# Four slot lanes by groups, rows of the second expert stage stored straight into the output, and places read when a block's rows arrive, in a conditioned transformer with two expert stages

## The chip, the cores and the metric

One Trainium2 chip, one of its cores. The metric is the device time of one execution in microseconds (us); lower is better. A core has TensorE (PE; PEld are its weight loads), VectorE (DVE), ScalarE (ACT), GpSimd (POOL) and SyncE (SP), which here only issues DMAs. Every engine works through its own instructions in order and waits on semaphores. Matrix products land in PSUM (the eight tensors `bank[0..7]`), everything else on chip is in SBUF (`sb_...`). All data is float32.

## The reference

Sixteen batch entries of 128 tokens with 128 features (2048 tokens, 16 tiles of 128x128).

```python
# layer 0: conditioned block, then experts
x = attention(adaln1(x)) + x ; x = cross_attention(adaln2(x), ctx) + x ; x = geglu(adaln3(x)) + x
z = layernorm(x); x = x + shared_ffn(z) + sum over the top 2 of 7 experts: w_k * ffn_k(z)
# layer 1: slot attention over the 77 context rows, 3 rounds, then experts
S = start from layernorm(x)                          # 128 slots per batch entry
for _ in range(3):
    q = layernorm(S); att = softmax over the slots; att = att / its row sums
    mid = S + update(att, values)                    # wu, bu
    S = layernorm(mid + w2 . gelu(w1 . layernorm(mid)) + ...)   # lnp_g, lnp_b
x3 = x + S ; z = layernorm(x3)
out = x3 + w * ffn_e(z), e the best of 8 experts, w its softmax share
```

## The kernel before

**Phase 1** (to about 550 us) runs layer 0's attention blocks as a software pipeline over the 16 tiles, iterations -1 to 17, stage B of tile b in iteration b + 1. The values of the cross attention go through DRAM: ACT fills `v2_rows`, SP stores them to `v2_all` (`store_values`) and loads tile b's part into `v2` (`load_values`), where PE waits for them in `pv_pair` by the semaphore `v2_in`. SP issues in program order, in the function `_(sp)`: the loads of inputs, `values(0)`, then two copies from DRAM to DRAM, `rows_a<-pad_a` and `rows_b<-pad_b`, that fill the tables of expert rows with padding, then `values(1)` to `values(15)`. In `load_values(b)` SP waits first until the stores it needs have landed. All these transfers are on SP's one queue.

**Stage a** (to 673 us): the first experts. Tokens are scattered to `rows_a` by expert; 38 blocks of 128 rows are loaded, multiplied, and sent back by `send_back("a", back_a)` on POOL. **Slots** (680 to 877 us): `back_a` is added to x, and the sixteen tiles go in two lanes of eight tiles (`LANES = ((0, 1), (2, 3))`, groups of four tiles), three rounds of `slot_round`. In a round DVE takes per lane statistics (`measured`: bn_stats, bn_aggr), POOL the power -1/2 (`root`), DVE the shift (`nbias`), ACT normalises (`normed`), PE turns the tiles (L893), ACT scales them (L1162), PE makes the logits (L903), DVE the maxima, ACT the exponentials (L1183), DVE the shares (L1748), PE the update (L911), DVE adds it (L1763), the same statistics and turn again, PE layer 1 (L923), ACT gelu (L1194), PE layer 2 (L929), DVE adds the rest (`mlp_sums`, L1783), measures and scales (`scaled`, L1713 and L1720). The order on each engine is that in which the calls stand in `slot_round`; PE, ACT, DVE and POOL run it in a hardware loop. POOL also keeps `s_rest` (L2057, L2063) and adds half of `back_a`.

**Routing b** (877 to 886 us): `routing("b", 0)` on DVE for all 16 tiles. POOL then scatters 16 tiles to `rows_b`, SP loads blocks. **Stage b** (910 to 963 us): 23 blocks: `turn_rows`, 4 products, ACT relu, 4 products, DVE bias (`leave`), and POOL in `send_back("b", back_b)`: `meta<-blk_x` (L2004), `dest<-meta` (L2011), an indirect DMA (L2016). **Tail**: SP loads `back_b` into `picked`, DVE multiplies by `wgt1` and adds x, SP stores `out`.

Of the kernel before, what the change touches and what calls it, by code (L numbers as in the profile page):

```python
# [32 lines left out]
NREG = EA * REGION + NR - 2 * TOK // P  # L33

PARTS = {"a": ((0, 12), (12, B)), "b": ((0, B),)}
SLOT_ITERS = 3
ROW = D + 2
NSLOT = 4
# [44 lines left out]

RANK_AT = [last + 2 for _, last in PARTS["a"][:-1]]

# [90 lines left out]
def program(nc, A, row_names, out):  # L176
    PLAN = proj_plan()
    with ExitStack() as ctx:
# [35 lines left out]
        start_a = sb("start_a", 1, NR, dt=I32)  # L214
# [63 lines left out]
        picked = sb("picked", P, B, 2, D)  # L278
# [6 lines left out]
        blk_x = sb("blk_x", P, NSLOT, ROW)  # L285
        meta = sb("meta", P, NR, 2)
        dest = sb("dest", P, NSLOT, dt=I32)
# [7 lines left out]

        rows_a = nc.dram_tensor("rows_a", (NREG * P, ROW), F32, kind="Internal").ap()
        rows_b = nc.dram_tensor("rows_b", (NB * P, ROW), F32, kind="Internal").ap()

        back_a = nc.dram_tensor("back_a", (2 * TOK + NREG * P, D), F32, kind="Internal").ap()
        v2_all = nc.dram_tensor("v2_all", (B * C, INNER), F32, kind="Internal").ap()  # L300
        back_b = nc.dram_tensor("back_b", (TOK + NB * P, D), F32, kind="Internal").ap()
# [19 lines left out]
        def quads(t):  # L321
# [25 lines left out]
        out_sem = sem("out_sem")  # L347
# [14 lines left out]
        meta_kept, dest_ready = ({x: sem(n + x) for x in "ab"} for n in ("meta_kept_", "dest_ready_"))  # L362
        sent_ready = sem("sent_ready")
# [9 lines left out]
        x2_step = sem("x2_step")  # L373
        sl_step, sl_var, sl_root = sem("sl_step"), sem("sl_var"), sem("sl_root")
        statq_ready, statm_ready, stat3_ready = (
            sem("sl_" + n) for n in ("statq_ready", "statm_ready", "stat3_ready"))
        zqT_done, zqT_ready, lg_done, nmax_ready, att_exp, att_ready, upd_done, mid_ready, mid_rest = (
            sem("sl_" + n) for n in ("zqT_done", "zqT_ready", "lg_done", "nmax_ready", "att_exp",
                                     "att_ready", "upd_done", "mid_ready", "mid_rest"))
        zmT_done, zmT_ready, hid_done, hid_ready, mlp_done, sum_ready, S_ready, S_rest = (  # L380
            sem("sl_" + n) for n in ("zmT_done", "zmT_ready", "hid_done", "hid_ready", "mlp_done",
# [12 lines left out]
        def tiles(lane):  # L394
            return range(4 * LANES[lane][0], 4 * LANES[lane][-1] + 4)
# [140 lines left out]
        def _(pe):  # L536
# [359 lines left out]
            def slot_logits(it, lane):  # L896
                for g in LANES[lane]:
                    turn_group(g, zq_ready, it * G + g + 1, zqT_done)
# [1259 lines left out]
```

## Time and profile before

| | us |
|---|---|
| median of 3 runs | 981.83 (980.21 to 982.06) |
| profiled execution: its time | 977.38 |
| its span, first to last instruction | 975.6 |
| busy: PE / DVE / ACT / POOL | 770.0 / 584.4 / 509.1 / 388.4 |
| chain that ended last, by engine | PE 46%, DVE 21%, issue 14%, POOL 9%, ACT 5% |

The span is the time from the first to the last instruction of the one profiled execution; 1.8 us of that execution lie around it. The chain that ended last is followed back from the last instruction, at each step to what released it.

### The profile page before, as it was taken

The page shows a single profiled execution, that of the slowest core. Times are in us where ns is not written, and L with a number is a line of the kernel's source. Part 1 is how long each engine was busy: PE and PEld are TensorE (multiplying, and loading weights), DVE is VectorE, ACT ScalarE, POOL GpSimd, SP SyncE. Part 2 cuts the span into 40 slices and gives each one's busy share as a digit, 9 for nine tenths or more (in the row PEclk, how much of TensorE's full clock was granted, in tenths as well). Part 3 has the DMA queues.
Part 4 walks back from the last instruction along what each step waited for, and adds up shares of the span by engine and source line. Part 5 has one row for each costly group of instructions (what it writes and reads, how often), then busy time and mean ns, then how long its engine had stood idle before and what let it go on. Part 6 is the DMA issues. An engine that isn't in the chain of part 4 may idle for free.

```text
span 975.6 us, 18523 instructions
## 1 busy us (share of the span) xinstructions
PE 770.0 (79%) x5945; PEld 650.1 (67%) x5945; DVE 584.4 (60%) x1939; ACT 509.1 (52%) x1078; POOL 388.4 (40%) x563
## 2 busy tenths in 40 slices
PE   5898899999999999999777699999363645550692
PEld 5677778788888788887665459998242534340692
DVE  2477778777767666568754443333869687763012
ACT  2566677666677666676444223335364545530461
POOL 1234354333333333332337333656624344225453
PEclk9799999999999999999897799999677677765796
DMA  9592011000011001010001136885300000002463
GB/s 264 182 352 94 1 36 36 14 23 28 2 35 36 15 16 34 2 35 28 14 6 37 68 99 174 253 244 167 106 1 1 0 0 0 0 1 76 127 198 106
DMA packets 43155, 70.95 MB, mean 73 GB/s; under 512 B 5339, under 2 KB 28587, under 8 KB 42651
## 3 DMA queue, kind: packets, MB, share of 16 engines
q1 hardware_dynamic: 39579, 62.64, 21.1%
q0 software_dynamic: 3488, 7.20, 2.1%
q8 instruction: 48, 0.79, 0.3%
q14 instruction: 40, 0.33, 0.1%
HBM read 56.53 MB, written 22.67 MB: 81 GB/s over the span
## 4 chain that ended last, share of the span: by engine, by line
PE 46%; DVE 21%; issue 14%; POOL 9%; ACT 5%; DMA 2%; SPq 2%; DVEq 0%; POOLq 0%; ACTq 0%
PE bank L568 5%; PE bank L839 5%; PE bank L630 5%; PE bank L593 3%; DVE sb_smax L1376 3%; PE bank L583 3%; DVE sb_row_sum L1386 3%; PE bank L618 3%; PE bank L574 2%; PE bank L602 2%; PE bank L847 2%; PE bank L659 2%; PE bank L970 2%; DVE sb_st_all L1680 2%; POOL sb_rstd_all L2052 2%
## 5 line engine op out<-in xcount | busy, mean ns | idle before, releaser
L1954 POOL TENSOR_TENSOR sb_expd<-sb_expd,sb_rden 128x512 f32<-128x512 f32 (+1 forms) x128 | 112.6, 880 | 270.3 <-DVE sb_rden L1390 270.1
L1376 DVE TENSOR_REDUCE sb_smax<-bank 128x4 f32<-128x512 f32 (+1 forms) x128 | 74.1, 579 | 63.6 <-PE bank L593 38.8
L618 PE MATMUL bank<-sb_eye,sb_expd 128*128 128x128 f32 (+1 forms) x512 | 78.2, 280 | 6.9 <-POOL sb_expd L1954 6.2
L1080 ACT ACTIVATE sb_expd<-sb_shifted 128x512 f32<-128x512 f32 (+1 forms) x128 | 69.8, 545 | 21.0 <-DVE sb_shifted L1379 19.6
L1386 DVE TENSOR_REDUCE sb_row_sum<-sb_expd 128x4 f32<-128x512 f32 (+1 forms) x128 | 72.9, 570 | 10.9 <-ACT sb_expd L1080 10.9
L1074 ACT ACTIVATE sb_probT<-bank 128x512 f32<-128x512 f32 (+1 forms) x128 | 74.3, 590 | 9.1 <-PE bank L618 8.8
L618 PEld LDWEIGHTS bank<-sb_eye,sb_expd 128*128 128x128 f32 (+1 forms) x512 | 59.9, 146 | 28.3 <-POOL sb_expd L1954 13.9
L1379 DVE TENSOR_TENSOR sb_shifted<-bank,sb_smax 128x512 f32<-128x512 f32 (+1 forms) x128 | 74.9, 585 | 4.4
L893 PE MATMUL bank<-sb_eye,sb_z_all 128*128 128x128 f32 x96 | 24.3, 420 | 66.9 <-ACT sb_z_all L1168 66.9
L568 PE MATMUL bank<-sb_h1T,sb_watt 128*128 128x128 f32 x512 | 72.6, 289 | 4.5 <-DMA sb_watt<-att_w 2.3
L630 PE MATMUL bank<-sb_probT,sb_v 128*64 128x128 f32 (+1 forms) x1024 | 71.2, 282 | 5.5 <-issue 4.0
L568 PEld LDWEIGHTS bank<-sb_h1T,sb_watt 128*128 128x128 f32 x512 | 64.6, 199 | 9.1 <-DVE sb_xb L1365 3.6
L1168 ACT ACTIVATE sb_z_all<-sb_S,sb_nbias,sb_rstd_all 128x128 f32<-128x128 f32 x84 | 33.6, 481 | 62.0 <-DVE sb_nbias L1707 62.0
L630 PEld LDWEIGHTS bank<-sb_probT,sb_v 128*64 128x64 f32 (+1 forms) x1024 | 55.6, 138 | 14.6 <-issue 5.4
L893 PEld LDWEIGHTS bank<-sb_eye,sb_z_all 128*128 128x128 f32 x96 | 17.5, 214 | 71.5 <-ACT sb_z_all L1168 71.2
L2052 POOL TENSOR_TENSOR sb_rstd_all<-sb_rsq_all,sb_halves 128x8 f32<-128x8 f32 x22 | 36.7, 1669 | 59.2 <-DVE sb_rsq_all L1695 59.1
L839 PE MATMUL bank<-sb_blk_xT,sb_up_w 128*128 128x128 f32 x456 | 57.1, 275 | 0.0
L839 PEld LDWEIGHTS bank<-sb_blk_xT,sb_up_w 128*128 128x128 f32 x456 | 54.0, 192 | 0.0
L2016 POOL DMA_INDIRECT back_a<-sb_blk_y,sb_dest x38 | 37.1, 976 | 40.0 <-DVE sb_blk_y L1657 21.7
L1648 DVE TENSOR_TENSOR sb_hid<-bank,sb_hid 128x384 f32<-128x384 f32 x38 | 21.2, 558 | 51.1 <-ACT sb_hid L1129 32.6
L602 PE MATMUL bank<-sb_g,sb_h2T 128*128 128x308 f32 x128 | 48.4, 461 | 0.0
L1659 DVE TENSOR_TENSOR sb_blk_y<-bank,sb_b2b 128x128 f32<-128x128 f32 x23 | 6.7, 291 | 64.0 <-PE bank L978 52.1
(251 smaller groups left out, 1886.9 us busy)
## 6 DMA issues: line engine op xcount, KB each, us to landing
sb_up_w<-gate_up SPq DMA_DIRECT2D x38, 384.0 KB
rows_a<-pad_a SPq DMA_DIRECT2D x1, 7670.0 KB, 26.8
sb_up_w<-w1b SPq DMA_DIRECT2D x23, 256.0 KB
sb_v<-v_all SPq DMA_DIRECT2D x16, 308.0 KB
v_all<-sb_v_rows SPq DMA_DIRECT2D x9, 512.0 KB, 2.6
sb_blk_x<-rows_a SPq DMA_DIRECT2D x38, 65.0 KB
sb_watt<-att_w SPq DMA_DIRECT2D x4, 512.0 KB, 6.3
sb_picked<-back_a SPq DMA_DIRECT2D x4, 512.0 KB, 5.4
```

Of the source, the lines that this page charges most:

```text
L568: mm = pe.matmul(t[:, c * n:(c + 1) * n], w[:, (4 * half + c) * P:(4 * half + c + 1) * P], src, start=True, stop=True)
L602: pe.matmul(score[u % 2][:, :, 0:C], h2T[:, :], g2[:, QH * j:QH * (j + 1), first:first + C], start=True, stop=True).then_inc(score_done, 1)
L618: mm = pe.transpose(trans[u % 2][0:n, h, :], expd[:, (units_before(i) + u) % EXP_RING, h, 0:n], eye[:, :])
L630: mm = pe.matmul(pvo[DH * r:DH * r + DH, h, :], v[:, 8 * (j // 2) + 2 * h + r, :], probT[0:n, (u - 1 + r) % 2, h, :], start=True, stop=True)
L839: mm = pe.matmul(bank[1 + 2 * j + v][:, c * P:(c + 1) * P], up_w[:, (u + 1) % NSLOT, (j * CA + c) * P:(j * CA + c + 1) * P], blk_xT[:, v, ...
L1074: act.activation(probT[0:n, u % 2, :, :], trans[u % 2][0:n, :, :], ACT.Copy).then_inc(probT_ready, 1)
L1080: act.activation(expd[:, (units_before(i) + u) % EXP_RING, :, 0:n], shifted[:, u % 2, :, 0:n], ACT.Exp, scale=DH ** -0.5).then_inc(exp_don ...
L1376: dve.tensor_reduce(smax[:, u % 2, :], s_in, X, ALU.max).then_inc(max_done, 1)
L1379: dve.tensor_tensor(shifted[:, u % 2, :, 0:n], s_in, smax[:, u % 2, :].unsqueeze(2).broadcast_to([P, QH, n]), ALU.subtract).then_inc(sub_d ...
L1386: dve.tensor_reduce(row_sum[:, u % 2, :], expd[:, (units_before(i) + u) % EXP_RING, :, 0:n], X, ALU.add).then_inc(row_sum_done, 1)
L1954: pool.tensor_tensor(e, e, rden[:, u % 2, :].unsqueeze(2).broadcast_to([P, QH, n]), ALU.mult).then_inc(norm_done, 1)
L2052: pool.tensor_tensor(rstd_all[:, c], rsq_all[:, 0, c], halves[:, c], ALU.pow).then_inc(sl_root, 1)
```

## The change

Five things. (1) The slot stage is unrolled and goes by four lanes of one group (four tiles) each. A table of numbers, `SLOT_STEPS`, gives each step a phase; step (iteration it, group g) stands at 4(it + 1) + g + phase, and every engine takes its steps in the order of these numbers (`slot_steps`). (2) What DVE added after layer 2 is now a product with `eye` that PE accumulates in PSUM (four more products per group and round); DVE measures and centres from PSUM; ACT normalises all groups; DVE adds all of `back_a`. (3) Routing b is done by group, and each group's rows are scattered when it is routed. (4) A row of `rows_b` now holds x3 and the weight as well (`ROW_B` = 258 numbers, was 130), and `rows_b` has a region for each expert: 135 blocks of rows (was 23), all filled from `pad_b`. DVE finishes a row in `leave` (bias, then weight and x3), POOL stores it with an indirect DMA into `out`; rows past the last token are dropped by a bounds check. The load of `back_b`, the last DVE sums and the stores of `out` are gone. (5) In both stages POOL takes a block's places into `dest` (now 8 deep) when the rows arrive, two blocks ahead, and in stage b copies 130 columns into `kept`.

```diff
-NREG = EA * REGION + NR - 2 * TOK // P
+NREG = {"a": EA * REGION + NR - 2 * TOK // P, "b": EB * REGION + NB - TOK // P}
+ROW_B = ROW + D
+SLOT_STEPS = {
+    range(0, SLOT_ITERS + 1): {"measure_q": -1.33, "root_q": -0.46, "shift_q": -1.09, "norm_q": -0.66, ...
...
-        rows_b = nc.dram_tensor("rows_b", (NB * P, ROW), F32, kind="Internal").ap()
+        rows_b = nc.dram_tensor("rows_b", (NREG["b"] * P, ROW_B), F32, kind="Internal").ap()
...
+                if step == "layer2":
+                    pe.wait_ge(mid_rest, nth(it, g))
+                    pe.wait_ge(hid_ready, nth(it, g))
+                    for n, b in enumerate(tiles(g)):
+                        pe.matmul(quads(bank[2 * g])[:, n, :], eye[:, :], s_rest[:, b, :], start=True, stop=False)
+                        mm = pe.matmul(quads(bank[2 * g])[:, n, :], hid[:, b, :], w2s, start=False, stop=True)
...
+            def measured(g, src, k):
+                stand()
+                for b in tiles(g):
+                    ins = dve.bn_stats(st_all[:, b, :], row(src, b))
+                link(ins)
+                stand()
+                for b in tiles(g):
+                    ins = dve.bn_aggr(mv_all[:, b, :], st_all[:, b, :])
+                link(ins)
...
+                if step == "gated":
+                    dve.wait_ge(lgb_done, g + 1)
...
+                if step == "choose":
+                    steps(of_b[g], 100)
+                if step == "place":
+                    steps(of_b[g], 100)
...
-                        pool.tensor_copy(dest[:, r:r + 1], meta[:, bass.ds(m, 1), 0:1].rearrange("p a n -> p (a n)")).then_inc(
-                            dest_ready[x], 1)
-                        pool.wait_ge(dest_ready[x], m + 1)
                         pool.wait_ge(y_ready[x], m + 1)
                         stand()
-                        pool.indirect_dma_start(dst, bass.IndirectOffsetOnAxis(ap=dest[:, r:r + 1], axis=0),
-                                                blk_y[:, r, :], None).then_inc(returned[x][r], 16)
+                        pool.indirect_dma_start(dst, bass.IndirectOffsetOnAxis(ap=dest[:, m % (2 * NSLOT):m % (2 * NSLOT) + 1], axis=0),
+                                                blk_y[:, r, :], None, **limit).then_inc(returned[x][r], 16)
...
+                if step == "send":
+                    pool.wait_ge(routed["b"], g + 1)
+                    for b in tiles(g):
+                        scatter_one("b", 0, b)
...
+            send_back("b", out_rows, bounds_check=TOK - 1, oob_is_err=False)
...
-            for g in range(G):
-                sp.wait_ge(out_ready, g + 1)
-                sp.dma_start(out[4 * g:4 * g + 4].rearrange("b s d -> s b d"),
-                             x_sb[:, 4 * g:4 * g + 4, :]).then_inc(out_sem, 16)
```

SP, in phase 1, before: the second store and the loads of values stand behind the two pads.

```order
L452 DMA v_all<-sb_v_rows 128x1024
L458 DMA sb_v<-v_all 77x1024
L469 DMA rows_a<-pad_a 128x15340
L469 DMA rows_b<-pad_b 32x11960
L452 DMA v_all<-sb_v_rows 128x1024
L458 DMA sb_v<-v_all 77x1024 x2
```

SP there now:

```order
L475 DMA v_all<-sb_v_rows 128x1024
L481 DMA sb_v<-v_all 77x1024
L492 DMA rows_a<-pad_a 128x15340
L492 DMA rows_b<-pad_b 288x15480
L475 DMA v_all<-sb_v_rows 128x1024
L481 DMA sb_v<-v_all 77x1024 x2
```

The order is the same; the second pad has 288x15480 numbers (17,415 KB) in place of 32x11960 (1,495 KB).

ACT, one round of the slots, before (the body of its loop; rows of the loop's own registers left out at both ends):

```order
L1183 ACTIVATE sb_att_or_sent,sb_esum<-bank,sb_nmax 77x128 x8
L1194 ACT_TABLE_LOAD
L1194 ACTIVATE sb_hid<-bank,sb_cols 128x512 x2
L1168 ACTIVATE sb_z_all<-sb_S,sb_nbias,sb_rstd_all 128x128 x8
L1162 ACTIVATE sb_zsT<-bank,sb_cols 128x512 x2
L1194 ACTIVATE sb_hid<-bank,sb_cols 128x512 x2
```

ACT now, one of the pieces that repeat in the middle of the slots, once for each group and round:

```order
L1169 ACT_TABLE_LOAD
L1169 ACTIVATE sb_att_or_sent,sb_esum<-bank,sb_nmax 77x128 x4
L1150 ACTIVATE sb_z_all<-sb_S,sb_nbias,sb_rstd_all 128x128 x8
L1156 ACTIVATE sb_zsT<-bank,sb_cols 128x512 x2
L1178 ACT_TABLE_LOAD
L1178 ACTIVATE sb_hid<-bank,sb_cols 128x512
```

The exponentials (L1169) of one group now stand between the gelus (L1178) of others, with a table load before each; before, a round had two loads. From the slots to the routing there are 22 loads, and there were 7.

DVE, at the end of the slots, now: the last group's shift, then the routing by group.

```order
L1654 SCALAR_TENSOR_TENSOR sb_nbias<-sb_mv_all,sb_rstd_all 128x4
L1721 TENSOR_TENSOR sb_logits<-bank,sb_rows 128x32
L1380 TENSOR_REDUCE sb_top<-sb_logits 128x4
L1382 TENSOR_TENSOR sb_rt<-sb_logits,sb_top 128x4x8
L1384 SCALAR_TENSOR_TENSOR sb_rt<-sb_rt,sb_rows 128x4x8
L1386 TENSOR_REDUCE sb_idx<-sb_rt 128x4
```

All four groups' routing, 87 instructions of 4 tiles and then 10 for the table of blocks, stands behind that shift; before, 28 instructions for 16 tiles did.

## Rows read from the trace of the kernel before

**Rows 1.** Stretches: length, busy us (instructions) of PE, PEld, DVE, ACT, POOL, granted clock, DMA share, GB/s
```profile
704.00:757.70 53.70, 28.89 (x140) 22.41 (x140) 42.43 (x200) 28.21 (x75) 20.28 (x14) 0.75 0.00 1
...
886.40:909.70 23.30, 0.00 (x0) 0.02 (x1) 0.81 (x3) 0.00 (x0) 15.41 (x16) 0.50 0.30 97
909.70:963.00 53.30, 47.02 (x391) 46.12 (x391) 6.70 (x23) 30.47 (x115) 28.94 (x68) 0.92 0.51 149
963.00:976.00 13.00, 0.00 (x0) 0.00 (x0) 4.38 (x16) 0.00 (x0) 0.97 (x1) 0.50 0.56 166
```

**Rows 2.** DMA issues and SP's timeline in phase 1: KB and landing; start, length
```profile
rows_a<-pad_a SPq DMA_DIRECT2D x1, 7670.0 KB, 26.8
rows_b<-pad_b SPq DMA_DIRECT2D x1, 1495.0 KB, 31.0
...
v_all<-sb_v_rows SPq DMA_DIRECT2D x1, 512.0 KB, 15.8
...
47.98 0.68 SPq L469 DMA_DIRECT2D rows_a<-pad_a  x1
...
65.11 0.33 SPq L452 DMA_DIRECT2D v_all<-sb_v_rows  x1
80.96 0.78 SPq L458 DMA_DIRECT2D sb_v<-v_all  x2
```

**Rows 3.** PE's timeline where tile 1's values are first used; a stretch after idle time
```profile
106.33 1.09 PE L630 MATMUL bank<-sb_probT,sb_v 77*64 77x128 f32 x16 [0.53 <-issue]
...
30.00:40.00 10.00, 10.00 (x83) 9.64 (x82) 5.05 (x10) 6.21 (x13) 2.70 (x3) 0.78 0.50 177
```

**Rows 4.** DVE's timeline in the slots: start, length of the piece
```profile
679.13 0.69 DVE L1832 TENSOR_TENSOR sb_x<-sb_x,sb_picked 128x512 f32<-128x512 f32 x1 [7.49 <-DMA sb_picked<-back_a]
...
766.27 1.13 DVE L1763 SCALAR_TENSOR_TENSOR sb_S<-bank,sb_rcol,sb_s_rest 128x128 f32<-128x128 f32 x4
...
769.27 1.64 DVE L1680 BATCH_NORM_STATS2 sb_st_all<-sb_S 128x6 f32<-128x128 f32 x8 [0.15 <-DVE sb_S L1763]
...
771.07 0.64 DVE L1686 BATCH_NORM_AGGREGATE sb_mv_all<-sb_st_all 128x2 f32<-128x6 f32 x8 [0.15 <-DVE sb_st_all L1680]
...
774.91 1.28 DVE L1737 TENSOR_REDUCE sb_lgmax<-bank 77x4 f32<-77x512 f32 x2
...
792.40 2.18 DVE L1713 SCALAR_TENSOR_TENSOR sb_S<-sb_S,sb_mv_all,sb_rows 128x128 f32<-128x128 f32 x8
...
861.62 2.19 DVE L1720 SCALAR_TENSOR_TENSOR sb_S<-sb_S,sb_rstd_all,sb_rows 128x128 f32<-128x128 f32 x8 [0.18 <-DVE sb_S L1713]
```

**Rows 5.** Groups of POOL by form, in phase 1: busy, mean ns
```profile
L1901 POOL TENSOR_TENSOR sb_rstd_all<-sb_rsq_all,sb_halves 128x4 f32<-128x4 f32 x6 | 6.1, 1021 | 6.2 <-DVE sb_rsq_all L1257 6.2
```

**Rows 6.** ACT's timeline in the slots
```profile
774.01 1.65 ACT L1168 ACTIVATE sb_z_all<-sb_S,sb_nbias,sb_rstd_all 128x128 f32<-128x128 f32 x4 [3.80 <-DVE sb_nbias L1707]
...
781.28 1.28 ACT L1194 ACT_TABLE_LOAD   x1
...
782.57 1.27 ACT L1194 ACTIVATE sb_hid<-bank,sb_cols 128x512 f32<-128x512 f32 x2
```

**Rows 7.** Timeline from the last shift to the first block of stage b
```profile
869.79 0.17 DVE L1707 SCALAR_TENSOR_TENSOR sb_nbias<-sb_mv_all,sb_rstd_all 128x8 f32<-128x8 f32 x1 [1.87 <-POOL sb_rstd_all L2052]
...
886.39 1.06 POOL L1924 DMA_INDIRECT rows_b<-sb_sent,sb_slot  x1 [16.59 <-DVEq L1506]
...
887.75 0.96 POOL L1924 DMA_INDIRECT rows_b<-sb_sent,sb_slot  x1 [0.30 <-issue]
...
909.71 0.45 PE L819 MATMUL bank<-sb_eye,sb_blk_x 128*128 128x128 f32 x1 [29.02 <-DMA sb_blk_x<-rows_b]
```

**Rows 8.** Timeline of stage b and of its end
```profile
919.19 0.97 POOL L2016 DMA_INDIRECT back_b<-sb_blk_y,sb_dest  x1 [0.82 <-POOL sb_dest L2011]
...
921.29 0.97 POOL L2016 DMA_INDIRECT back_b<-sb_blk_y,sb_dest  x1 [0.82 <-POOL sb_dest L2011]
...
965.51 2.03 SPq L526 DMA_DIRECT2D sb_picked<-back_b  x4
```

More of the change, by code:

```diff
@@ L397, in program, with tiles @@
+        def tiles(g):
+            return range(4 * g, 4 * g + 4)
         NBLK = {"a": NR, "b": NB}
@@ L497, in load_weights, with load_blocks @@
                     up_w_in[m % NSLOT], 16)
-            def load_blocks(x, src, scatters, place):
+            def load_blocks(x, src, scatters):
                 sp.wait_ge(table_ready[x], 1)
-                places = [place(m) for m in range(NSLOT)]
+                places = [place(x, m) for m in range(NSLOT)]
                 for m in range(NSLOT):
@@ L508, in load_blocks @@
                 for m in range(NSLOT, NBLK[x]):
-                    first, e = place(m)
+                    first, e = place(x, m)
                     load(x, src, m, first)
@@ L956, in _ @@
+                if step == "gate":
+                    pe.wait_ge(zT_ready["q"], nth(it, g))
+                    for n, b in enumerate(tiles(g)):
+                        mm = pe.matmul(bank[2 * g + 1][:, n * EB:(n + 1) * EB], zsT[:, b, :], wgate[:, :], start=True, stop=True)
+                    mm.then_inc(lgb_done, 1)
+                if step == "rank":
+                    rank_sums("b", g, bank[2 * g])
+            pe.wait_ge(ranks_kept["b"], G)
             pe.wait_ge(ld_moe_b, 32)
@@ L1643, in step_a @@
                 if exists(n - 1, NR):
[L1644 to L1645 removed]
+                    leave("a", q, u, bank[6 + v])
                 if exists(n + 1, NR):
@@ L1849, in _ @@
[L1849 to L1859 removed]
+                if step == "measure_m":
+                    dve.wait_ge(mid_ready, nth(it, g))
+                    measured(g, S, "m")
@@ new lines, in _ @@
+                if step == "shift_m":
+                    shifted_by(it, g, "m")
+                if step == "measure_o":
+                    if it >= 0:
+                        dve.wait_ge(mlp_done, nth(it, g))
+                    measured(g, x_sb if it < 0 else SUMS, "o")
+                if step == "centre":
+                    scale = es_b[:, :] if it < 0 else R["lnp_g"]
+                    src = x_sb if it < 0 else SUMS
+                    for b in tiles(g):
+                        ins = dve.scalar_tensor_tensor(S[:, b, :], row(src, b), mv_all[:, b, 0:1], scale, ALU.subtract, ALU.mult)
+                    link(ins)
```

615 lines of the change are left out of this document (223 added, 392 removed).

## The prediction

> **What bounds the kernel now.** I read the stretches by stage first, then for each stage the timeline of the engine that is full. Phase 1 and stage a are TensorE's. In a slot round of 53.7 us no engine is full: DVE is busy 42.4, PE 28.9, ACT 28.2, POOL 20.3, and DMA nothing [rows 1]: two lanes are too few to cover the way from engine to engine, so DVE stands still a fifth of the time. Then PE, ACT and DVE do next to nothing for 23 us while POOL scatters 16 tiles [rows 1, 7]. Stage b goes at POOL's pace, one indirect DMA every 2.1 us [rows 8], with PE busy 47.0 of 53.3. In the last 13 us only rows move [rows 1]. These four places are what the change works on. SP's timeline in phase 1 shows a fifth that it works on as well: the store of tile 1's values, issued at 65.11, took 15.8 us to land, because the two pads were in front of it on SP's queue, and the loads could be issued only at 80.96 [rows 2].
>
> **The pads: +31.6.** They are issued at 47.98 and 48.7 and land after 26.8 and 31.0 us, at 74.8 and 79.7: the 1,495 KB of the second took 4.9 us, 305 KB each us [rows 2]. The new second pad has 135 x 128 rows of 258 numbers, 17,415 KB, so 15,920 KB more: 52.2 us at that rate, 55.6 at the rate of the first pad alone (7,670 KB in 26.8 us). The store landed at 80.9, 1.2 us behind the pad; behind the new one it lands at about 133, and the load, of which the trace shows no landing and for which I take 2 us, at 135. PE first needs those values at 105.8: it starts on them at 106.33 after 0.53 us idle [rows 3]. Before, that left 105.8 - 83.0 = 22.8 us of cover. All of it goes: 52.2 - 22.8 = 29.4 us in which PE stands in its order at `pv_pair`, and with it everything that phase 1 feeds. PE is the full engine there, so nothing gives this back later. After an idle time the granted clock comes back late: in the ten microseconds from 30 on PE was busy throughout at a mean clock of 0.78 [rows 3], which is 2.2 us of work lost. I take 29.4 + 2.2. The ends: 25 if the copies run a tenth faster, 35 by the slower rate. The Trainium skill, DMA: Bandwidth & Descriptors, Specifications, gives a limit of about 358 GB/s for a core's HBM; by that the extra pad would take about 45 us and the whole would come to 967. The trace shows less than that rate, and the sum goes by the trace.
>
> **Stage a: -0.5.** Places are read early, so POOL's last DMA no longer waits 0.82 us behind its cast (as in [rows 8]); the blocks before it are hidden behind PE.
>
> **The slots: -21.8.** What DVE does for one group in one round, from [rows 4]: the update 1.13 and a short reciprocal, 1.3; three measures, each four bn_stats (half of 1.64), four bn_aggr (half of 0.64), two waits of 0.15 and a short one, 1.55 each, 4.65; centring and scaling half of 2.18 and of 2.19 with a wait, 2.4; maxima half of 1.28 and two short ones, 1.15; shares, four instructions like the update's, 1.1; two shifts, 0.2. That is 10.8 us. The other way round: 42.4 busy in a round [rows 1], less four sums (0.65 each, as the maxima read a bank) and the four normalisings (1.1) is 38.7, 9.7 a group, plus some seven waits of 0.15: the same. bn_stats and centring now read PSUM, which no row shows for bn_stats; the update reads PSUM at the price of the centring that reads SBUF (1.13 for four against 2.18 for eight), so I take nothing, with +0.3 a group as the other end. The power of four columns takes 1.02 [rows 5]. With four lanes DVE should be nearly full. I take 11.1 for a unit (one group's share of a round), since a few waits must stay.
>
> By the order that the table gives, DVE begins at 679.13 [rows 4] and has until the first unit in which everything runs: eight sums of 0.84, 6.7; four times a measure, centring, scaling and a measure, 22; three maxima 3.4, two updates 2.6, two measures 3.1, two shares 2.1, shifts 0.5: 40.4 us. Then 8.45 full units, 93.8. Then three units that grow thinner: 11.6, 9.4, and 6.5 plus 3.1 in which DVE waits for the last group's way through ACT, PE and POOL; the last measure with its sum 2.5 and its power 1.5. Together 168.8, so the last shift is at 847.9; it was at 869.79 [rows 7].
>
> **Routing and scatters: -5.6.** All 87 small instructions of the routing come after that shift. At 0.22 us they take 19, with waits for ranks 22; that is longer than the 15.7 us from the last shift to the last place before. But the first group's places are ready 6 us after the shift, and POOL scatters from then on: 16 DMAs at 1.27 (0.96 and a gap of 0.30, [rows 7]) and four leads of 1 us, 24.3. DVE's next group takes 5.7, POOL's 6.1, so POOL sets the pace and the last DMA starts at 847.9 + 6 + 24.3 - 1 = 877.2. It started at 887.75 + 14 x 1.26 = 905.4: 28.2 earlier, of which 21.9 are the slots'. The rows are twice as long, for which I give 0.7 back.
>
> **Stage b: -2.5.** Each block now costs POOL a copy of 130 columns instead of 2, the same cast, and the DMA without the wait for that cast. What the 0.82 us before the DMA [rows 8] is made of decides: between scatters that wait for nothing it is 0.30 [rows 7]. If it falls to that, a block takes about 1.7 on POOL and PE is the bound, at most 53.3 - 47.0 = 6.3 us saved; if the 0.82 stays and the copy adds 0.1, 23 blocks cost 2 more. I take the middle. **The tail: -9.6.** The last rows used to be back when SP loaded them at 965.51 [rows 8]; the 10.1 us behind that are gone, and DVE's second instruction in `leave` puts 0.5 in.
>
> **Sum:** 31.6 - 0.5 - 21.8 - 5.6 - 2.5 - 9.6 = -8.4 on the profiled execution's 977.4 us (span 975.6). The median of the runs was 981.8, 4.4 above that execution, so 973.4; I say 974.
>
> **The rivals.**
> *ACT becomes the bound in the slots (chance 0.2, about 986, slower).* Its unit has eight normalisings (two of 1.65), two scalings 1.6, four exponentials 1.5, a gelu 0.64 and now two table loads of 1.28 [rows 6]: 9.6 of DVE's 11.1. In the trace the gelu starts 0.01 us after the load's end, at 782.57, so nothing is hidden in it. But if a load also costs the wait until the chain before it is through, say its own length again, ACT's unit is 12.2, and DVE, which waits for the exponentials and the gelu of each group, follows: 1.1 x 8.45 and 3 in the thin units, +12.3. It decides from a unit of 12.1 on, where the gain of 8.4 is gone. The Trainium skill, ScalarE: Activation LUTs, What ACT_TABLE_LOAD costs, says that every switch costs about 1.38 us of drain besides 1.28; by that the unit is 12.4 and the time about 988. The trace, with 0.01 us behind the load, does not agree, and so the chance stays at 0.2.
> *The pads cost less (0.15, about 956).* Either the store gets through beside them or the copy runs faster. For it: the descriptors are new in shape. Against: the store's 15.8 us. With half the stall the time is 974 - 16 = 958; with none 942.
> *Stage b does not get shorter, or the long copy and rows make it longer (0.15, about 980).* POOL at 2.3 us a block gives +2 to +4 instead of -2.5. Or the slots' unit is 11.6 by PSUM reads: +4.
> *As summed (0.5): 966 to 982.*
>
> **How the numbers follow.** The likeliest case gives 974. What is measured from run to run is about 0.2%, 2 us. Faster by more than that: nearly all of the pads' rival, four fifths of the summed case, half of stage b's: 0.15 + 0.4 + 0.08 = 0.63, and 0.02 from the others. Slower: ACT's 0.2 less what stays short, and the summed case's upper edge, 0.24. Same: 0.11. The range leaves out no stall at all and the worst of ACT's case: 955 to 989.
>
> **What the profile after would show.** The second pad landing 80 to 87 us after its issue, SP's second loads at about 133, PE idle for about 29 us before the first products of `probT` with tile 1's values (L630 before); a DVE unit of 11.1 us, so that the same step of one group comes back every 44.4; ACT at under 90% in the slots with gaps below 0.1 behind table loads; the scatters beginning in four bunches before the routing ends; blocks of stage b under 2.0 apart; nothing behind the last DMA into `out`. I am wrong if PE does not wait in phase 1 (then 30 us better), or if DVE waits for ACT's exponentials or gelus in every unit (then no gain).

## The result and the profile after

The changed kernel takes 1005.41 us in the median (1002.09 to 1006.59) against 981.61 before on the same chip: a ratio of 1.0247, interval 1.0227 to 1.0266, 2.5% slower. I had said 974. Its profiled execution took 1002.09 us with a span of 1000.3, 24.7 longer than before.

I cut both spans at the same six events; the starts of before are in [rows 4], [rows 7] and [rows 8].

| stretch | before | after | change | predicted |
|---|---|---|---|---|
| start to the first addition of the slots | 679.1 | 704.1 | +25.0 | +31.1 |
| first addition to last shift | 190.7 | 197.3 | +6.6 | -21.8 |
| last shift to first product of stage b | 39.9 | 38.4 | -1.5 | -5.6 |
| first product to POOL's last DMA | 53.4 | 50.3 | -3.1 | -2.5 |
| that DMA to the end | 12.5 | 10.2 | -2.3 | -9.6 |

The changes add up to 24.7. The one large miss is the slots, 28 us; the small ones (6 too much for the pads, 7 too much gained in the tail, 4 in the routing, under 1 in stage b), with their signs, come to 5 together. The stretches after the change, a unit (one group's share of a round) in the second row, as in [rows 1]:

```profile
704.10:901.40 197.30, 115.40 (x599) 95.59 (x597) 164.95 (x732) 118.80 (x271) 75.27 (x68) 0.72 0.07 20
...
771.90:785.36 13.46, 8.42 (x43) 6.96 (x42) 11.33 (x52) 9.23 (x22) 5.52 (x5) 0.75 0.00 1
```

In a unit DVE is busy 11.33 of 13.46 us. Of the 11.33, 1.6 are time that two instructions take longer than they need, as the next timeline shows; without it DVE's work is 9.8, and I had counted 9.7. So neither the amount of work nor a full DVE explains 13.46.

The pads, as in [rows 2] and [rows 3]: first the DMA issues (landing in us), then SP's timeline and PE's where tile 1's values are first used.

```profile
rows_b<-pad_b SPq DMA_DIRECT2D x1, 17415.0 KB, 80.1
...
62.77 0.33 SPq L475 DMA_DIRECT2D v_all<-sb_v_rows  x1
127.80 0.73 SPq L481 DMA_DIRECT2D sb_v<-v_all  x2
...
131.51 1.98 PE L641 MATMUL bank<-sb_probT,sb_v 77*64 77x128 f32 x16 [24.91 <-DMA sb_v<-v_all]
```

SP's second store of values waits behind the long pad, its loads are issued 65 us later, and PE stands 24.9 us. Everything downstream starts 25.0 us later.

One unit of the slots on DVE, as in [rows 4], and the two long additions of POOL in it:

```profile
771.77 1.13 DVE L1694 SCALAR_TENSOR_TENSOR sb_S<-bank,sb_rcol,sb_s_rest 128x128 f32<-128x128 f32 x4 [0.20 <-DVE sb_rcol L1690]
...
776.04 0.94 DVE L1648 TENSOR_SCALAR sb_rsq_all<-sb_mv_all 128x4 f32<-128x4 f32 x1
...
778.33 1.67 DVE L1685 TENSOR_SCALAR sb_att_or_sent<-sb_att_or_sent,sb_rsum 77x128 f32<-77x128 f32 x4
...
784.96 0.24 DVE L1690 RECIPROCAL sb_rcol<-bank 128x2 f32<-128x2 f32 x2 [1.20 <-PE bank L919]
785.23 0.35 DVE L1694 SCALAR_TENSOR_TENSOR sb_S<-bank,sb_rcol,sb_s_rest 128x128 f32<-128x128 f32 x1
...
775.70 1.26 POOL L1925 TENSOR_TENSOR sb_s_rest<-sb_S,sb_cb 128x512 f32<-128x512 f32 x1
778.05 1.27 POOL L1921 TENSOR_TENSOR sb_s_rest<-sb_S,sb_rows 128x512 f32<-128x512 f32 x1
```

The same step comes back after 13.46 us. Before that DVE waits 1.2 us for PE's update, and two instructions are long: L1648 takes 0.94 where it takes 0.17 elsewhere in the unit, L1685 1.67 where four such (L1748) take 0.87 in the trace of before. Both run under an addition of POOL. What holds the unit together is seen in the chain that ended last, of which this is one turn (start, length, what):

```profile
776.90 0.16 DVE sb_nbias L1654
...
777.08 1.66 ACT sb_z_all L1150 x4
...
778.78 1.12 PE bank L905 x4
779.90 1.71 PE bank L914 x8
781.61 1.71 PE bank L926 x2
783.31 1.63 PE bank L919 x8
...
784.96 0.04 DVE sb_rcol L1690
```

It goes round in nearly every unit: DVE's update of group g, its measure and another group's, the shift (L1654), ACT's normalising (L1150), PE's turn of the same tiles (L905), and only behind that turn, because the table says so, PE's logits (L914), layer 1 (L926) and the update (L919) of group g + 1, for which DVE waits.

The end of the slots and the routing, as in [rows 7]:

```profile
901.39 0.16 DVE L1654 SCALAR_TENSOR_TENSOR sb_nbias<-sb_mv_all,sb_rstd_all 128x4 f32<-128x4 f32 x1 [1.24 <-POOL sb_rstd_all L1910]
...
908.93 0.21 DVE L1469 TENSOR_REDUCE sb_top<-sb_hot 128x4 f32<-128x32 f32 x1 [2.11 <-ACT sb_hot L1182]
...
931.56 0.96 POOL L1785 DMA_INDIRECT rows_b<-sb_picked_or_sent,sb_slot  x1 [0.30 <-issue]
933.28 1.97 SPq L516 DMA_DIRECT2D sb_up_w<-w1b  x4
935.44 5.36 SPq L508 DMA_DIRECT2D sb_blk_x<-rows_b  x5
...
939.81 0.45 PE L831 MATMUL bank<-sb_eye,sb_blk_x 128*128 128x128 f32 x1 [16.02 <-DMA sb_blk_x<-rows_b]
```

The scatters do run in four bunches, the last one 30.2 us behind the last shift (35.6 before). But the table of blocks is now made behind the last group's places, so SP issues four loads of weights (1 MB) in front of the first rows: 8.3 us from the last scatter to the first product, 4.3 before.

And the end, as in [rows 8]: POOL's last DMA, and the instruction in POOL's queue that closes the program (its lengths and its start):

```profile
990.11 0.98 POOL L1880 DMA_INDIRECT out<-sb_blk_y,sb_dest  x1 [0.71 <-issue]
...
L203 POOLq DRAIN  x1: 10183/10183/10183, 989.9 to 989.9; - x1
```

SP has seen the last rows land by 992.3. Nothing but this drain runs until 1000.1. The same instruction in the trace of before:

```profile
L178 POOLq DRAIN  x1: 10181/10181/10181, 962.9 to 962.9; - x1
```

There it was over at 973.1, under the loads and stores of the tail that the change takes away.

### The profile page after: what moved, and what is told of

Read it like the earlier page. It is cut to its first block, busy times and chain, and to the rows that moved or that the text cites. A ratio compares the mean times of both kernels' runs of the same rounds, so it can differ in the third digit from the quotient of the medians.

```text
span 1000.3 us, 18890 instructions
## 1 busy us (share of the span) xinstructions
PE 793.0 (79%) x6053; PEld 671.9 (67%) x6053; DVE 611.6 (61%) x2039; ACT 536.3 (54%) x1112; POOL 394.2 (39%) x584
## 4 chain that ended last, share of the span: by engine, by line
PE 50%; DVE 19%; issue 9%; another core or an unknown queue 6%; ACT 6%; POOL 4%; SPq 2%; DMA 2%; DVEq 0%; POOLq 0%; ACTq 0%
PE bank L851 5%; PE bank L641 5%; PE bank L579 5%; PE bank L604 3%; PE bank L594 3%; DVE sb_st_all L1641 3%; DVE sb_smax L1341 2%; PE bank L859 2%; PE bank L629 2%; PE bank L585 2%; PE bank L812 2%; PE bank L957 2%; DVE sb_row_sum L1351 2%; PE bank L613 2%
## 5 line engine op out<-in xcount | busy, mean ns | idle before, releaser
L641 PE MATMUL bank<-sb_probT,sb_v 128*64 128x128 f32 (+1 forms) x1024 | 73.8, 289 | 29.5 <-DMA sb_v<-v_all 24.9
L1910 POOL TENSOR_TENSOR sb_rstd_all<-sb_rsq_all,sb_halves 128x4 f32<-128x4 f32 x44 | 45.6, 1036 | 122.4 <-DVE sb_rsq_all L1648 121.1
L905 PE MATMUL bank<-sb_eye,sb_z_all 128*128 128x128 f32 x96 | 22.6, 378 | 68.8 <-ACT sb_z_all L1150 68.8
L905 PEld LDWEIGHTS bank<-sb_eye,sb_z_all 128*128 128x128 f32 x96 | 14.5, 189 | 74.4 <-ACT sb_z_all L1150 67.9
L1150 ACT ACTIVATE sb_z_all<-sb_S,sb_nbias,sb_rstd_all 128x128 f32<-128x128 f32 x96 | 39.5, 486 | 28.8 <-DVE sb_nbias L1654 28.8
L1075 ACT ACTIVATE sb_oTB<-bank 128x512 f32<-128x512 f32 x32 | 19.1, 597 | 60.6 <-PE bank L641 60.6
## 6 DMA issues: line engine op xcount, KB each, us to landing
rows_b<-pad_b SPq DMA_DIRECT2D x1, 17415.0 KB, 80.1
```

The lines of the kernel that those rows point to most:

```text
L641: mm = pe.matmul(pvo[DH * r:DH * r + DH, h, :], v[:, 8 * (j // 2) + 2 * h + r, :], probT[0:n, (u - 1 + r) % 2, h, :], start=True, stop=True)
L1910: pool.tensor_tensor(rstd_all[:, c], rsq_all[:, 0, c], halves[:, c], ALU.pow).then_inc(root_ready[k], 1)
```

## Experiments

I give each kernel's ratio to the kernel before, run beside it on the same chip; in it 0.01 is 9.8 us. The changed kernel's own is 1.0247. The second expert stage is called stage b, as ahead.

**The pad in pieces.**

```diff
-            for t, pad in ((rows_a, A["pad_a"]), (rows_b, A["pad_b"])):
-                sp.dma_start(*(v.rearrange("(p n) d -> p (n d)", p=P) for v in (t, pad))).then_inc(zeroed, 16)
+            sp.dma_start(*(v.rearrange("(p n) d -> p (n d)", p=P) for v in (rows_a, A["pad_a"]))).then_inc(zeroed, 16)
             for i in range(1, B):
                 values(i)
+                piece = slice(9 * (i - 1) * P, 9 * i * P)
+                sp.dma_start(*(v[piece].rearrange("(p n) d -> p (n d)", p=P) for v in (rows_b, A["pad_b"]))).then_inc(zeroed, 16)
```

POOL's wait for the pads, ahead of its first scatter, counts the sixteen copies.

> The changed kernel, but the second pad goes in 15 pieces of nine blocks of rows (1,161 KB, by the changed kernel's 17,415 KB in 80.1 us some 5.3 us each), one behind each load of values. Theory (the pad in front of tile 1's values holds PE for 24.9 us and nothing gives it back): SP's second loads at about 81 as before the change, PE idle under 1 us before the first products with tile 1's values, the first addition of the slots at 679 to 681 instead of 704.1, and 980 us in all (25 less). Rival (phase 1 has the slack to give part of it back, or the pieces delay later values): less than 20 us gained, with waits of PE on loads of values later in phase 1.

Measured: 979.34 us, ratio 0.9959 (0.9939 to 0.9978): 28 us less than the changed kernel, and already a little faster than before. PE's timeline at the same products:

```profile
106.42 1.09 PE L642 MATMUL bank<-sb_probT,sb_v 77*64 77x128 f32 x16 [0.54 <-issue]
```

The stall is gone to the 0.5 us it was before [rows 3]. The first addition is at 684.5, not at 680, but this profiled execution was the slowest of the ten, 3.4 us above their median. Such times vary: with the long pad unchanged the first addition is at 704.1 in the changed kernel and at 709.1 with the update first (the next run), and most of that lies in the wait itself, 24.9 and 28.8 us. So the ratio is the better measure: 28 us, give or take 3. The rival falls.

**Is it the order on PE, or ACT's table loads?** Three kernels: one number of the table, no table loads (the identity in place of gelu, which is left out), and both.

```diff
-    ... "shares": 0.48, "update": 1.43, "updated": 0.89,
+    ... "shares": 0.48, "update": 0.73, "updated": 0.89,
```

> The changed kernel with one number of the table changed: the phase of the update on PE is 0.73 instead of 1.43, so PE makes the update of the next group before it turns this group's tiles for layer 1. Theory A (the unit of 13.45 us is a circle through engines that work in order: DVE's update of group g, its two measures, ACT's normalising, PE's turn, and only behind that turn, the logits and layer 1 PE's update of group g + 1, which DVE waits for): the circle is cut, the unit falls to 11.3 to 11.8 and the time by some 17 to 22 us, to about 986. Theory B (ACT with its two table loads per group is the limit): the unit stays at 13.4 and the time at 1005. Theory C (POOL's work slows DVE, which is the limit): DVE has under 0.5 us of waits per unit already, and the time changes by less than 4.

```diff
-                    act.activation(group_of(hid, g), bank[2 * g + 1][:, :], ACT.Gelu, bias=sb1_).then_inc(hid_ready, 1)
+                    act.activation(group_of(hid, g), bank[2 * g + 1][:, :], ACT.Identity, bias=sb1_).then_inc(hid_ready, 1)
```

> The changed kernel, with the identity in place of gelu in the slots (the hidden layer is computed differently), so that ACT has one function family there and no table load between exponentials and gelus: 2.56 us less on ACT per group and round. Theory A (circle through the order, on which no gelu, exponential or table load lies): the unit stays at 13.2 to 13.5 and the time within 3 us of 1005. Theory B (ACT with its table loads is the limit): the unit falls by about 2.5 us to 10.9 and the time by some 22, to about 983.

> Both edits: PE's update at phase 0.73, and the identity in place of gelu in the slots (the hidden layer is computed differently). Theory A: once the circle is cut DVE is the limit, so that taking the table loads away as well adds little, under 0.4 us per unit, and the time is that of the kernel with the earlier update less 0 to 4. Theory B: the time is that of the kernel without table loads, about 983, whatever the order on PE. If the two edits are worth more together than the sum of each alone, the table loads are next in line behind the circle.

Measured: the update first 1020.85 us, ratio 1.0391 (1.0352 to 1.0430), 14 us *slower*; no tables 1006.81, 1.0238 (1.0202 to 1.0274), no change, with 198.2 us from the first addition to the last shift (197.3); both 1019.44, 1.0376 (1.0334 to 1.0417), as the first alone. So table loads are not the limit with either order: theory B falls. So does theory C in its strong form, since DVE waits 1.2 us a unit for PE, though POOL's part comes up again below. Theory A's forecast of the gain, 17 to 22 us, falls too. The chain of the first kernel shows why:

```profile
788.05 2.09 PE bank L919 x8
790.14 0.85 PE bank L905 x4
790.99 1.71 PE bank L914 x8
792.70 1.72 PE bank L926 x2
794.44 0.70 ACT sb_hid L1178
...
795.28 0.46 PE bank L931 x2
```

The old circle is cut, and another has closed behind it: DVE's shares, PE's update, turn, logits and layer 1, ACT's gelu, PE's layer 2, DVE's measure of that sum, shares again; 14.2 us (DVE takes up the update at 779.77, 793.99, 808.21). POOL is on this one too: DVE's shares (L1685) take 1.66 us in it, not 0.87. One step moved by feel opened one circle and closed a longer one.

**Does PE's length make the circle?** The changed order, with half the columns of three products left out:

```diff
-                        mm = pe.matmul(quads(bank[2 * g + 1])[0:C, n, :], kq[:, b, :], zsT[:, b, :], start=True, stop=True)
+                        mm = pe.matmul(quads(bank[2 * g + 1])[0:C, n, 0:64], kq[:, b, :], zsT[:, b, 0:64], start=True, stop=True)
...
-                    pe.matmul(bank[2 * g + 1][:, :], w1s, flat(zsT, g), start=True, stop=True).then_inc(hid_done, 1)
+                    pe.matmul(bank[2 * g + 1][:, 0:256], w1s, flat(zsT, g)[:, 0:256], start=True, stop=True).then_inc(hid_done, 1)
```

and the update alike, on columns 65 to 128 of 129.

> The changed kernel in its own order, but PE's logits, layer 1 and update in the slots work on half their columns (the other half of these products is left out, so the numbers are not the reference's). Theory A2 (the table would do if PE's products took half as long; at the granted clock of 0.75 of these units, mostly its lower level, they make the circle longer than DVE's work): three products on the circle lose 0.85 us each, 2.6 together, and the unit falls from 13.45 to DVE's own 11.2 to 11.6, the time by 18 to 22. Rival (PE's length is not on the circle; the waits come from table loads or from POOL): under 5 us gained.

Measured: 993.28 us, ratio 1.0123 (1.0098 to 1.0148), 12 us less; slots 186.3 us, unit 12.2. Its chain, at the turn of the circle:

```profile
791.27 1.12 PE bank L905 x4
792.39 1.01 PE bank L914 x8
793.41 1.07 PE bank L926 x2
794.48 1.60 PE bank L919 x8
...
796.18 0.23 DVE L1690 RECIPROCAL sb_rcol<-bank 128x2 f32<-128x2 f32 x2
```

Logits went from 1.71 to 1.01 and layer 1 from 1.71 to 1.07, the update stayed at 1.60: 1.3 us less, and the unit is 1.3 shorter. So PE's length stands on the circle, but my 2.6 us was twice what the halving gave. The last row, from DVE's timeline, has no wait for PE any more: DVE is busy 11.2 of the 12.2 us, and L1648 and L1685 are still long (0.94 and 1.67). With those two as they are, DVE's own limit is 12.2, not 11.2. The changed kernel's own trace agrees. Its unit from 798.51 to 810.71 is 12.2 us too: from 809 to 812 the granted clock is 1.00, the update takes 1.06, and DVE does not wait for it.

```profile
809.36 1.06 PE L919 MATMUL bank<-sb_vu,sb_att_or_sent 77*128 77x129 f32 x8
...
810.71 0.23 DVE L1690 RECIPROCAL sb_rcol<-bank 128x2 f32<-128x2 f32 x2
```

**All numbers of the table anew.** I replayed the order of each engine with the lengths of the steps as the changed kernel's trace has them, and looked for numbers with which no circle is longer than DVE's own work. The second set:

```diff
+    (-1,): {"add": 1.13},
+    range(0, SLOT_ITERS + 1): {"measure_q": -0.29, "root_q": -0.04, "shift_q": -0.03, "norm_q": -0.78,
+        "turn_q": 0.01, "scale_q": -0.26},
+    range(SLOT_ITERS): {"logits": 0.7, "max": 0.6, "exp": -0.07, "shares": 0.74, "update": 0.87, "updated": 1.22,
+        "keep_mid": 1.96, "measure_m": 1.29, "root_m": 1.6, "shift_m": 1.42, "norm_m": 1.21, "turn_m": 1.96,
+        "scale_m": 1.7, "layer1": 2.55, "gelu": 1.75, "layer2": 2.71},
+    range(-1, SLOT_ITERS): {"measure_o": 2.98, "root_o": 3.28, "centre": 3.02, "slots": 3.37},
+    range(-1, SLOT_ITERS - 1): {"keep_slots": 3.7},
...
```

> The changed kernel with all numbers of its table chosen anew, with the lengths of the steps as its trace shows them (PE at its slow clock: 1.7 us for logits, layer 1 and update, 2.1 for layer 2, 0.9 for a turn), so that no engine stands before a step whose input comes round through three others. Theory A (the order makes the circle, and each order has its own: 13.45 us with the changed kernel's, 14.2 with the update ahead): the unit falls to 11.2 to 11.6, where DVE's 11.2 to 11.6 busy us per unit are the limit, and the time by 18 to 22 us, to about 985. Rival (with PE at its slow clock no order of four lanes gets below 13): less than 5 us gained.

Measured: 997.92 us, ratio 1.0174 (1.0153 to 1.0194): 7 us less, a third of what I expected; unit 12.68, slots 191.5. DVE waits for neither PE nor ACT in it. DVE's and POOL's timelines of one unit show what it does wait for:

```profile
787.33 1.14 DVE L1654 SCALAR_TENSOR_TENSOR sb_nbias<-sb_mv_all,sb_rstd_all 128x4 f32<-128x4 f32 x1 [0.23 <-POOL sb_rstd_all L1910]
788.40 0.68 DVE L1678 TENSOR_REDUCE sb_lgmax<-bank 77x4 f32<-77x512 f32 x1
789.11 0.58 DVE L1679 SCALAR_TENSOR_TENSOR sb_nmax<-sb_lgmax,sb_kqb 77x4 f32<-77x4 f32 x1
...
787.18 1.28 POOL L1921 TENSOR_TENSOR sb_s_rest<-sb_S,sb_rows 128x512 f32<-128x512 f32 x1
788.41 1.27 POOL L1925 TENSOR_TENSOR sb_s_rest<-sb_S,sb_cb 128x512 f32<-128x512 f32 x1
```

A shift of four columns lasts 1.14 us and ends at 788.47; POOL's addition ends at 788.46. L1679 ends at 789.69; POOL's second addition at 789.68. L1678, which reads PSUM, is not lengthened (0.68). The Trainium skill, SBUF — State Buffer, SBUF: two separate sides, says that VectorE and GpSimd take one shared pair of ports as an exclusive lock for a whole instruction, on VectorE's side for operations with two SBUF inputs or in a two-port mode. The rows agree: the shift and L1679 have two inputs in SBUF. In the changed kernel L1648 and L1685 (TENSOR_SCALAR) lost 0.8 us each; they read one tensor in SBUF, and that they run in a two-port mode no row here shows. The 0.8 of L1648 stands on the circle there, just ahead of the shift at 776.90.

**The collision by itself, and avoided.** The second set, with three quarters of POOL's two additions left out:

```diff
+                    w = 4 if it < 0 else 1
-                    pool.tensor_tensor(group(s_rest, g), group(S, g), R["bu"].unsqueeze(1).broadcast_to([P, 4, D]),
+                    pool.tensor_tensor(group(s_rest, g)[:, 0:w, :], group(S, g)[:, 0:w, :], R["bu"].unsqueeze(1).broadcast_to([P, w, D]),
```

and the addition of `cb2` alike.

> The kernel with the second set of numbers, but POOL's two additions of 512 columns per group and round cover 128 columns (three quarters of the rest's update are left out), so that each lasts about 0.4 us instead of 1.27. Theory H (DVE's small instructions wait for POOL's addition to end): the shift and L1679 last under 0.4 us, the unit falls from 12.68 to 11.3 to 11.8, and the time by 10 to 14 us from 998. Rival (those instructions are long for another reason, such as their own inputs from POOL): unit 12.5 or more, under 3 us gained.

Measured: 984.08 us, ratio 1.0047 (1.0030 to 1.0064), 12.5 us less than with the second set, in the same order; slots 179.2, unit 11.43, the shift 0.33. The third set of numbers keeps POOL's additions whole and puts them elsewhere:

```diff
+    range(0, SLOT_ITERS + 1): {"measure_q": 0.32, "root_q": 1.92, "shift_q": 0.46, "norm_q": -0.92,
+        "turn_q": 0.05, "scale_q": -0.75},
+    range(SLOT_ITERS): {"logits": 0.2, "max": 0.99, "exp": -0.04, "shares": 1.34, "update": 0.68, "updated": 1.72,
+        "keep_mid": 3.3, "measure_m": 1.74, "root_m": 3.55, "shift_m": 1.96, "norm_m": 1.03, "turn_m": 2.04,
+        "scale_m": 1.23, "layer1": 2.2, "gelu": 1.89, "layer2": 2.45},
+    range(-1, SLOT_ITERS): {"measure_o": 3.64, "root_o": 4.93, "centre": 3.7, "slots": 3.87},
+    range(-1, SLOT_ITERS - 1): {"keep_slots": 6.28},
...
```

> The changed kernel with a third set of numbers in its table. The second set gave a unit of 12.68 us, in which DVE's chain has no wait for PE or ACT left; 1.4 us of it are two small DVE instructions that last until POOL's addition of 512 columns ends (the shift 1.14 instead of 0.16, L1679 0.58 instead of 0.16). The new order keeps the additions on POOL under DVE's instructions that were not lengthened (bn_stats, bn_aggr, those that read PSUM). Theory H (the collision with POOL is worth 1.4 us a unit, and behind it DVE's own 11.2 are the limit): unit 11.2 to 11.6, last shift 170 to 176 us behind the first addition instead of 197.3, and about 980 to 985 us in all. Rival (something else fills the room: the unit stays above 12.4): no better than the second set's 998.

Measured: 981.88 us, ratio 1.0018 (1.0004 to 1.0032), 22.5 us less than the changed kernel; slots 174.1 us, unit 11.3. DVE and POOL, one unit:

```profile
758.02 0.87 DVE L1641 BATCH_NORM_STATS2 sb_st_all<-sb_S 128x6 f32<-128x128 f32 x4
...
760.96 0.16 DVE L1654 SCALAR_TENSOR_TENSOR sb_nbias<-sb_mv_all,sb_rstd_all 128x4 f32<-128x4 f32 x1 [0.24 <-POOL sb_rstd_all L1910]
...
757.96 1.26 POOL L1925 TENSOR_TENSOR sb_s_rest<-sb_S,sb_cb 128x512 f32<-128x512 f32 x1 [0.21 <-DVE sb_S L1694]
```

POOL's addition lies under bn_stats, which is not lengthened (0.87 either way), and the small ones are 0.16 again. DVE is busy 10.0 us of the 11.3. Theory H holds in both.

**Rows in front of weights in stage b.**

```diff
-                for m in range(NSLOT):
-                    load_weights(x, m, places[m][1])
+                if x == "a":
+                    for m in range(NSLOT):
+                        load_weights(x, m, places[m][1])
                 sp.wait_ge(scattered[x], 16 * scatters)
                 for m in range(NSLOT):
                     load(x, src, m, places[m][0])
+                    if x == "b":
+                        load_weights(x, m, places[m][1])
```

> The changed kernel, but in the second expert stage SP issues the first four loads of rows each in front of its load of weights, instead of behind all four loads of weights. Theory (the table of blocks comes at 930.2 now, at the end of all routing, so that 1 MB of weights stands in front of the rows: rows are issued at 935.4 and the first product is at 939.8, 8.3 us behind the last scatter's issue, where before it was 4.3): the first product comes 2 to 4 us earlier and the time falls by 2 to 3 us. Rival (the scatters' landing sets the start, or the weights are then late): under 1 us.

Measured: 1002.46 us, ratio 1.0215 (1.0194 to 1.0236), 3 us less, give or take 3; the rows say the same. From the last scatter (937.53 here) to the first product (942.61) it is 5.1 us instead of 8.3.

**What ends the program.** In the first kernel POOL waits for all its landings and copies one column:

```diff
             send_back("b", out_rows, bounds_check=TOK - 1, oob_is_err=False)
+            for u in range(NSLOT):
+                pool.wait_ge(returned["b"][u], 16 * len(range(u, NB, NSLOT)))
+            pool.tensor_copy(kept[:, 0, 0:1], zeros[:, 0:1])
```

> The changed kernel, but POOL waits at its end until its own last DMA has landed (at 992.3 by SP's wait) and then copies one column. Its last instruction, the drain at the end of the program, lasts 10.18 us in both traces, from 962.9 before and from 989.9 after the change, and ends the span of the changed kernel alone. Theory F (the drain has a fixed length on POOL): it starts at about 992.6 and still lasts 10.2, and the span grows by 2.7 us. Theory G (the drain lasts until something that the DMA began is over): it ends at the same time as in the changed kernel and is 7.5 us long or less, with no change of the time.

The second leaves the last 8 of the 23 blocks unsent:

```diff
+        SENT = {"a": NR, "b": 15}
...
-                    if exists(m, NBLK[x]):
+                    if exists(m, SENT[x]):
```

> The changed kernel, but the last 8 of the 23 blocks of the second expert stage are not sent into the output (their rows are left out); POOL still copies their places and rows when they arrive. In the changed kernel nothing runs from 992.3 to 1000.1 but POOL's drain, which ended 8.98 us behind POOL's last instruction there and 8.95 behind it in the kernel that waited for the landing. Theory F (the program ends 9 us behind POOL's last instruction of any kind): that one is now a copy at about 985, the drain ends at 994 to 995, and the time falls by 5 to 6. Theory G (9 us behind its last DMA): that one is at about 975, the drain is over before DVE ends at 989, and the time falls by 9 to 11. Rival (the last blocks' landing in DRAM sets the end, not the drain): the time falls by less than 2.

Measured: 1004.23 us, ratio 1.0241 (1.0218 to 1.0264), for the first, no change that can be told; 994.99 us, 1.0169 (1.0140 to 1.0197), 8 us less, for the second. The last work on POOL and the drain, in the first and in the second:

```profile
993.45 0.19 POOL L1937 COPY sb_kept<-sb_zeros 128x1 f32<-128x1 f32 x1 [1.33 <-DMA out<-sb_blk_y,sb_dest]
...
L203 POOLq DRAIN  x1: 9177/9177/9177, 993.4 to 993.4; - x1
```

```profile
982.29 0.19 POOL L1875 CAST sb_dest<-sb_blk_x 128x1 int32<-128x1 f32 x1
...
L203 POOLq DRAIN  x1: 8642/8642/8642, 982.2 to 982.2; - x1
```

The drain ends 8.9 us behind the copy in the first, although all of POOL's DMAs had landed before it, and 8.4 behind the cast in the second, 14.8 behind the last DMA's end. In the changed kernel and in the one before it is 9.0. So it is theory F, though not to the tenth: where nothing else runs longer, the program ends 8.4 to 9.0 us behind POOL's last instruction of any kind. My number for the second run was wrong, since I had POOL's last copy at 985 (it comes two blocks ahead, at 982.5). The fall of the time, 8 us give or take 3, does not decide between F and G; the rows do. In the first run the end came 11.7 us behind the start of the last DMA instead of 10.2: 1.5 more, less than the 2.7 expected, because the recorded 10.18 begin ahead of that DMA (989.9 against 990.11) and only 9.0 of them lie behind its end.

**All that paid, in one kernel**: the third set, the pad in pieces, rows in front of weights, and

```diff
+                    if nth(it, g) == SLOT_ITERS * G:
+                        act.activation(warm[:, :], sb1_, ACT.Exp)
```

behind the last gelu.

> Everything that paid or should pay, in one kernel: the third set of numbers, the pad in 15 pieces behind the loads of values, the first rows of the second expert stage in front of their weights, and an exponential of one column behind the last gelu, so that the table for the choice's exponentials is loaded while ACT waits. From the changed kernel's 1005: 25 for the pad, 20 to 25 for the order (if the third set does as expected), 3 for rows and weights, 1.3 for the table: 951 to 957, faster than before by 2.5 to 3%. If the gains overlap (phase 1 does not give all of the pad's 25, or the routing behind the slots waits for something else) 960 to 965.

Measured: 952.23 us (950.90 to 954.83), ratio 0.9725 (0.9705 to 0.9745): 2.75% faster than before and 5% faster than the changed kernel. Its slots take 175.4 us, and POOL's last DMA stands 10.2 us ahead of the end, as after the change. The table load now lies at 845.94, where ACT waits; the first scatter comes 10.3 us behind the last shift all the same (8.6 after the change), since in this order DVE chooses for three groups before it places the first; it waits for no exponential now, but what the load is worth was not seen by itself.

## Why the prediction was wrong, point by point

- **The pads, +31.6: right in mechanism, 6.6 too large in the profiled execution.** Store, loads and wait came as written. The extra 15,920 KB took 49.1 us (80.1 against 31.0), not 52.2; and the pads were issued 2.3 us earlier in this execution, so they ended earlier against PE's first use. The 2.2 for the clock do not show: PE's first products behind the wait take 1.98 instead of 1.09, but they start 25.2 us later than before and the first addition 25.0. The wait is 24.9 here, the shortest of the eleven traces that have the long pad in front (up to 29.2, their middle one 27.8), and by the ratio of the kernel without it 28, give or take 3. My 29.4 for the wait was nearly right.
- **Stage a, -0.5:** lost in the 5 us by which that stretch varies.
- **The slots, -21.8: wrong, and this is the step that decided.** "With four lanes DVE should be nearly full. I take 11.1 for a unit, since a few waits must stay." DVE's amount was right: with an order that lets it, the unit is 11.3. What failed is that I took DVE's own work as the unit and put two things at nothing without a reason. The first is the circle. I never walked the order of the table through the other engines with their lengths in the trace: PE makes the update of g + 1 behind the turn of g, the turn waits for DVE by way of ACT, and three products on the way last 1.7 us each. The granted clock is 0.50, the lower of the two levels, from 778 to 784, under these products, and 1.00 from 772 to 777, where PE has little to do; eight products of L957 in stage b take 1.92 us each time at 0.50 and 1.06 at 1.00. The circle is 13.46. Most of DVE's and ACT's members stood in [rows 4] and [rows 6]; PE's I had not taken from the trace. The second is POOL's additions holding up DVE's instructions, 1.6 us a unit. The trace of before did show it, and I read the wrong row: the scaling that [rows 4] has at 2.19 us (861.62) is the last round's, where POOL adds nothing. In the other rounds the same eight instructions take 3.20 to 3.22, over POOL's addition.

```profile
794.82 3.22 DVE L1720 SCALAR_TENSOR_TENSOR sb_S<-sb_S,sb_rstd_all,sb_rows 128x128 f32<-128x128 f32 x8 [0.23 <-DVE sb_S L1713]
...
796.04 1.32 POOL L2057 TENSOR_TENSOR sb_s_rest<-sb_S,sb_rows 128x512 f32<-128x512 f32 x1 [1.80 <-DVE sb_S L1720]
```

In numbers: the slots take 197.3 us, 186.3 with PE's products cut (POOL's holds still there) and 174.1 with the third set, against my 168.8. So the circle is 11 us of the 28, the holds about 12, and some 5 are the sum itself, its start and end and 0.2 in each unit.

- **The rival I gave a chance of 0.2 had the right sign for the wrong reason.** I named ACT's table loads, at 986; without any of them the time is the same (1.0238 against 1.0247). The Trainium skill's drain at each switch (ScalarE: Activation LUTs, What ACT_TABLE_LOAD costs), by which I had worked out 988, does not show either: here the load starts 0.01 us behind the gelu's end (784.04) and the exponential 0.02 behind the load's. The gelu before it, 1.33 us behind its own load, waits for layer 1.

```profile
784.05 1.28 ACT L1169 ACT_TABLE_LOAD   x1
785.35 0.36 ACT L1169 ACTIVATE sb_att_or_sent<-bank,sb_nmax 77x128 f32<-77x128 f32 x1
```

- **Routing and scatters, -5.6: measured -1.5.** The last scatter did move by 5.5 us, where my steps gave 6.3. What I left out is behind it: the table of blocks is made last, so weights stand in front of the rows, 4.0 us, of which turning them gave back 3. And the first scatter came 8.6 us behind the last shift, not 6: DVE waits 2.11 us for an exponential behind its table load.
- **Stage b, -2.5: measured -3.1.** POOL's DMAs are 1.93 us apart (22 steps in 42.5 us) instead of 2.10. I had taken the middle of two cases, so that it fits is in part luck; PE is busy 47.6 of the 50.3 us, so the case in which PE sets the pace came, with half its gain.
- **The tail, -9.6: measured -2.3.** I took the last rows to be the bound and missed that POOL's drain ran underneath until 973.1 of a span of 975.6. With the drain where it was, taking the tail away could gain 2.5 at most.

## What to carry to other kernels

An order written as a table is a set of circles: before counting an engine as full, follow from each of its waits back through every in-order engine to its own previous unit, with the lengths and the clock the trace shows at that place; moving one step can close a longer circle (here 13.46 became 14.2). Where the same instruction has two lengths in a trace, as 2.19 and 3.22 here, find out what runs beside the long one before taking the short one into a sum. Before taking a stretch away at the end, look at what else was running under it, drains in the queues too. A long DMA that nobody waits for still belongs behind the short ones that somebody does.

## What the runs showed that I had not expected

- POOL's drain at the end of the program: it ends 8.4 to 9.0 us behind POOL's last instruction in four kernels, whereas in the changed kernel the same instruction takes 0.81 us on ACT, 0.39 on DVE and 0.01 on SP.
- A DVE instruction of four columns with its two inputs in SBUF, 0.16 us alone, lasts until POOL's addition of 512 columns ends (1.14 us); bn_stats (0.87), bn_aggr (0.38) and a maximum that reads PSUM (0.68) keep their lengths under such an addition.
- Halving the columns of a product of 129 hardly shortened it: the eight updates took 1.60 us for 64 columns (granted clock 0.50) and 1.63 for 129 (0.58 in the mean), whereas eight logits fell from 1.71 to 1.01, both at 0.50. Why is not shown.
